# Wide attentions of a four-layer transformer trunk on one core: a batch's output projection a slot later, values made ahead of turning the outputs

## The reference

```python
def _L1_xattn_ref(q, kv, Wq, Wk, Wv, Wo, bo):
    qh = (q @ Wq).reshape(B, N, NUM_HEADS, HEAD_DIM).transpose(0, 2, 1, 3)
    kh = (kv @ Wk).reshape(B, M, NUM_HEADS, HEAD_DIM).transpose(0, 2, 1, 3)
    vh = (kv @ Wv).reshape(B, M, NUM_HEADS, HEAD_DIM).transpose(0, 2, 1, 3)
    attn = jax.nn.softmax(jnp.einsum('bhnd,bhmd->bhnm', qh, kh) * scale, axis=-1)
    out = jnp.einsum('bhnm,bhmd->bhnd', attn, vh)
    return out.transpose(0, 2, 1, 3).reshape(B, N, INNER) @ Wo + bo

def _mha(x, y, ..., causal):                      # layer 2, twice
    xn, yn = _ln(x, lnx_g, lnx_b), _ln(y, lny_g, lny_b)
    a = jax.nn.softmax(jnp.einsum('bhsd,bhtd->bhst', q, k) * D ** (-0.5), axis=-1)
    if causal:
        a = a * (jnp.arange(t)[None, :] > jnp.arange(s)[:, None])
    o = jnp.einsum('bhst,bhtd->bhsd', a, v)
    x_out = x + o.transpose(0, 2, 1, 3).reshape(..., H * D) @ li1_w + li1_b
```

## Time and profile before

| | |
|---|---|
| time, median of 3 runs | 1491.01 us (1490.46 to 1492.49) |
| time of the profiled execution | 1502.04 us |
| its span, first to last instruction | 1500.3 us |
| mean granted clock of TensorE | 0.812 of full speed |
| busy: PE, DVE, ACT, POOL | 1046.5, 916.3, 693.2, 628.5 us |
| L1x, L2a1, L2a2 in the span | about 283 to 496, 602 to 809, 864 to 1037 us |

### The profile page before, as it was taken

One profiled execution on the slowest core, in us unless ns is written; L12 is line 12 of the kernel. 1 busy time (PEld: TensorE's weight loads), 2 busy tenths in 40 slices (PEclk: granted clock), 3 DMA queues, 4 the chain that ended last, 5 costly groups with the idle time before them and its releaser, 6 DMA issues.

```text
span 1500.3 us, 37065 instructions
## 1 busy us (share of the span) xinstructions
PE 1046.5 (70%) x14701; PEld 800.4 (53%) x14748; DVE 916.3 (61%) x2387; ACT 693.2 (46%) x1356; POOL 628.5 (42%) x575
## 2 busy tenths in 40 slices
PE   0477777688888454688885678886827992667674
PEld 0355566456677243366673447674516781445564
DVE  5567554677765694789865566653615456767443
ACT  2546454565553442554433455543514553555321
POOL 3355724164343333355342245442144036655333
PEclk9768588899999675799975868995857995678797
DMA  6533132110010100000000000000022123332122
GB/s 167 140 111 94 59 81 69 38 43 21 23 31 9 33 16 32 19 16 10 3 3 35 2 1 3 3 3 1 1 69 64 52 62 109 106 111 77 48 66 79
DMA packets 68790, 71.54 MB, mean 48 GB/s; under 512 B 11598, under 2 KB 51918, under 8 KB 68430
## 3 DMA queue, kind: packets, MB, share of 16 engines
q1 hardware_dynamic: 64528, 60.77, 14.2%
q0 software_dynamic: 4096, 8.40, 1.9%
HBM read 44.90 MB, written 23.59 MB: 46 GB/s over the span
## 4 chain that ended last, share of the span: by engine, by line
PE 48%; DVE 26%; ACT 9%; issue 7%; POOL 4%; DMA 3%; POOLq 2%; SPq 1%; ACTq 0%; DVEq 0%
PE psum L631 20%; PE psum L1100 6%; PE psum L1118 5%; DVE area L1699 5%; PE psum L750 5%; PE psum L740 4%; ACT area L1189 2%; PE psum L638 2%; POOL sorted_in L2563 2%; ACT xn L1211 2%; DVE area L1805 2%; DVE negm L1798 2%; DVE stats L1680 2%; POOLq L2373 1%; DVE area L1909 1%
## 5 line engine op out<-in xcount | busy, mean ns | idle before, releaser
L1189 ACT ACTIVATE area<-psum 128x512 bf16<-128x512 f32 (+4 forms) x288 | 148.2, 543 | 225.6 <-PE psum L785 103.2
L1699 DVE TENSOR_TENSOR area<-psum,area 128x512 bf16<-128x512 f32 (+3 forms) x280 | 163.2, 622 | 43.8 <-ACT area L1189 43.0
L2434 POOL TENSOR_TENSOR area<-area 77x1024 bf16<-77x1024 f32 x64 | 121.6, 1916 | 98.3 <-ACT area L1322 98.3
L631 PE MATMUL psum<-area 77*128 77x65 bf16 (+4 forms) x3712 | 133.8, 189 | 22.2 <-DVE area L2093 21.6
L1322 ACT ACTIVATE area<-psum 77x1024 f32<-77x1024 f32 (+1 forms) x96 | 97.7, 1021 | 103.0 <-PE psum L750 102.8
L1798 DVE TENSOR_REDUCE negm<-psum 128x4 bf16<-128x308 f32 (+1 forms) x192 | 95.5, 539 | 80.6 <-PE psum L723 80.6
L631 PEld LDWEIGHTS psum<-area 77*128 77x128 bf16 (+2 forms) x3712 | 124.7, 104 | 29.9 <-issue 25.0
L2292 DVE TENSOR_TENSOR area<-area 128x512 bf16<-128x512 f32 x106 | 73.1, 691 | 108.7 <-ACT area L1595 79.7
L1100 PE MATMUL psum<-xT_hi,moe 128*128 128x128 bf16 x848 | 110.3, 228 | 15.7 <-DVE xT_lo L1699 11.6
L638 PE MATMUL psum<-wide,xn 128*128 128x128 f32 x144 | 32.2, 367 | 113.2 <-ACT xn L1211 100.5
L2392 POOL TENSOR_TENSOR moe<-stage,moe 128x512 bf16<-128x512 f32 x47 | 55.5, 1183 | 131.6 <-ACT moe L1184 131.4
(11 more groups left out here) (226 smaller groups left out, 2619.3 us busy)
## 6 DMA issues: line engine op xcount, KB each, us to landing
area<-keys_dram SPq DMA_DIRECT2D x24, 320.0 KB, 5.0
area<-sorted_in SPq DMA_DIRECT2D x22, 256.0 KB, 3.6
sorted_out<-area SPq DMA_DIRECT2D x22, 256.0 KB
keys_dram<-area SPq DMA_DIRECT2D x8, 640.0 KB, 3.0
stage<-in_w_L0m SPq DMA_DIRECT2D x16, 256.0 KB, 2.9
stage<-in_w_L2m SPq DMA_DIRECT2D x16, 256.0 KB, 2.7
stage<-in_w_L3m SPq DMA_DIRECT2D x16, 256.0 KB, 3.0
area<-queries_dram SPq DMA_DIRECT2D x24, 128.0 KB, 2.6
```

The costliest lines, as they stand in the source:

```text
L631: ins = pe.matmul(out, lhsT, rhs, start=i == 0, stop=i == len(terms) - 1)
L1189: ins = act.activation(out, bank, ACT.Copy)
L1699: ins = dve.tensor_tensor(out, bank, high, ALU.subtract)
L2434: pool.tensor_tensor(A.PL[n % 4][0:A.L], A.PF[n % 4][0:A.L, :].rearrange("p (h q) -> p h q", h=8), A.PH[n % 4][0:A.L], ALU.subtract).then_ ...
```

## The change

In the wide attentions the output projection of a batch is issued one slot later, behind the first pair of row maxima, and the last one behind the loop; the values are made (TensorE) and split (ScalarE, VectorE) ahead of the turned outputs. In VectorE's program of L2a1 the values also come ahead of the low half of the first exponentials. GpSimd's and SyncE's programs are as they were.

```diff
@@ tensor_program, attention @@
             if b < B:
                 row_maxima(b, (0, 1))
+            if b >= 5:
+                out_project(b - 5)
             if 0 <= b - 3 < B:
                 outputs(b - 3)
+            if 0 <= b - 1 < B:
+                values(b - 1)
             if b >= 4:
                 turn_outputs(b - 4)
-            if 0 <= b - 1 < B:
-                values(b - 1)
             if b < B:
                 row_maxima(b, (2, 3))
             if ahead < NG and b % GB >= 1:
                 for kind, tile in A.jobs_at(b):
                     project(ahead, kind, tile)
-            if b >= 4:
-                out_project(b - 4)
             if ahead < NG and b % GB == 0:
                 group_turned(ahead)
             if ahead < NG and b % GB == 1:
                 keys_turned(ahead)
+        out_project(B - 1)
         end()
```

## The result

The changed kernel took 1508.36 us (median of 4 runs, 1504.94 to 1511.07) against 1491.75 for the kernel before (1490.46 to 1495.17): a ratio of 1.0107, 95% interval 1.0075 to 1.0138. It is 16.6 us slower, where 6.3 us of gain were forecast. The profiled execution is its fastest, 1504.94 with a span of 1502.9. The order of TensorE, VectorE and ScalarE moved as the diff says; L631, L638, L723, L740 and L785 keep their numbers, the others stand one or two further down: `copy_hi` is L1190, `split_lo` L1700, xn L1212, the maxima L1799, the exponentials' low half L1806, GpSimd's mask L2444.

What follows compares the result with a forecast made beforehand. Bound: TensorE and VectorE handing work to and fro, neither full. -(3.2 + 1.2 + 2.6) - 2.7 + 5.9 - 2.7, given as -6.3, took the median of 1491.0 to 1484.7 us; range 1476 to 1495.

Steps and rivals of the forecast that it cites:

- rival 4: Whole kernel: slower because TensorE's clock falls to 1.2 GHz behind stalls, 2.2 us a drop; chance 0.17.
- six turning slots: Slots b = 4 and 8 of the three wide attentions, each forecast to stall 1.3 to some 2 us.
- The term of 5.9: Slots b = 4 and 8: the projection no longer covers ScalarE's late xn; 5.9 us lost (2.1 + 2.3 + 1.5).
- 2.2 a drop: Price of one clock fall, read from an L2a1 slot at 0.55 that took 11.36 us against 9.17.
- Ordinary slots: b = 12 to 15, without projections: gains of 3.2 us in L2a2, 1.2 in L1x, 2.6 in L2a1.
- M: Second pair of maxima; in L1x forecast still to wait about 0.75 to 0.8 us for the values' second low half.
- the loop through GpSimd: L2a1's ordinary slots: outputs, low halves, exponentials and masks form a binding loop of 8.8 us, down from 9.17.
- T in L1x: Turning of batch b-4's outputs; its first low half, ending 1.97 us after its products begin, was applied to L2a1's values.
- b = 16: Slot without maxima: waits of 1.13 us in L2a2, 0.86 in L1x and 0.7 in L2a1 vanish; sum 2.7.
- The wait for xn: Turning of xn at b = 4 and 8: TensorE waits for ScalarE's normalised xn, 1.3 us (L1x) to some 2.
- Slots with projections: Wide attentions: L1x 0, L2a2 gains 1.4 us, L2a1 1.3 at b = 5 and 9; -2.7 in all.

## Why the prediction was wrong

**The step that failed** is the weighing of rival 4. The prediction had written the mechanism and its outcome with all six turning slots, 1498, and gave it 0.17, because "1.50 in every slot of L2a1 did not bring it in the 106 us ahead of it". That took a wait that VectorE had imposed in ten slots as a proof that TensorE may stand still so long anywhere. So the sum held the clock at nothing. The runs showed otherwise: L2a2's b = 9 took 14.18 behind a wait of 2.14 and 9.32 without it, with the wait for xn gone 29 us come back, and with the wait filled 18. The term of 5.9 for the slots that turn the next group was right for L1x's and L2a2's b = 8, left out what follows them, and was 3.6 too small for L2a1's b = 8 alone (13.79 against 9.66, 0.5 forecast), which had a clock of 0.62.

Rival 4 was nearer, but it too tied the falls to the six waits for xn. The measured 1508.36 is above its 1498, and part of the time at the lower level stands elsewhere: L2a1's b = 3 (0.51) comes ahead of its first such wait, the fall in b = 8 ahead of the second, and b = 14 to 16 (0.83 to 0.86) six slots and more behind the last. With the swap alone the clock fell with no wait for xn at all, and with the projection's move alone the kernel is not slower. A small slip stands beside this: the terms of the sum add up to -6.5, not -6.3.

**Its size** was off too. "2.2 a drop" was read from a slot of L2a1 (11.36 against 9.17) in which TensorE had 1.5 of waiting to give up to the lower clock. L2a2's b = 9 holds projections and had 8.4 of work in 9.74, so half the clock cost 4.4; L1x's b = 9 lost 1.5 (15.05 against 13.53), with a clock of 0.89.

The Trainium skill, TensorE: Matmul & The Clock Gate, section "HAM oscillation", lets the clock fall behind idle gaps; L2a2's b = 9 agrees, though the gap of 2.14 there is shorter than the waits of the section's example (3 to 5 us, for a DMA). L2a1's b = 8, at 0.50 with no wait above 0.91 in the 10 us ahead of it, does not show such a gap.

**Ordinary slots.** L2a2: 6.56 with no wait, forecast 6.6. L1x: 9.44 with 0.85 ahead of M, forecast 9.43 and 0.75 to 0.8. Both right, 4.6 us of gain (4.4 forecast). L2a1: the loop through GpSimd binds and TensorE waits 1.02 inside the outputs, as said, but the loop is 9.16 and not 8.8. The terms of it that were too small: V's low half ends 2.22 behind the start of its products (756.03 to 757.56 + 0.69), where I took 1.97 from T in L1x, since V is three products summed in one bank and ScalarE starts 0.90 behind the first, not 0.72; some 0.1 more lies in two hand-overs between VectorE and GpSimd. Besides, b = 12 took 8.52, not 7.67. So the new order won 0.7 there instead of 2.6 even at full clock, and b = 14 and 15 (10.27 and 10.00) were not at full clock. The second exponentials ended 1.08 behind the mask that they met (753.51 against 752.43), the length taken from the earlier trace rows; by the full block of the Trainium skill's SBUF — State Buffer, "SBUF: two separate sides", it would have been 1.21, and here as there the row is a little shorter.

**b = 16**: 6.19 in L2a2 against 8.15 (the wait of 1.13 gone, most of the rest a stretch at the lower level in the kernel before), 8.03 in L1x against 9.07, a gain of 1.04 where 0.86 was forecast. Near enough there; in L2a1 9.28 against 9.23, with 2.6 us at the lower level, so nothing of the 0.7.

**The wait for xn**: 1.34 in L1x (forecast 1.35), 2.14 in L2a2, 2.08 in L2a1; L1x's and L2a2's slot 8 longer by 1.06 (11.28 against 10.22) and 0.87, forecast 1.05 and 0.95. Right to a tenth in these two.

**Slots with projections** (forecast -2.7): L2a2's b = 6, 7, 10 and 11, at full clock, were shorter by 0.18, 0.46, 0.16 and 0.17, and b = 9, where xn early kept the clock up, by 0.42: 1.4, as forecast. L2a1 won nothing on the whole: b = 3 took 11.53 against 9.88 before, b = 9 with xn early 12.13 against 12.54, b = 10 11.43 against 11.10. That b = 3 is ahead of any turning and is 9.88 again once the exponentials' low half goes first. The swap has a part in it, which I had put at zero: b = 2 took 11.96 in all profiles with the values ahead of the exponentials, 10.85 in most of the others, and b = 3 was at 0.51 behind it. But with the projection's move alone b = 3 was at 0.57 too (11.19), so that the swap is not shown to be the only cause.

**What is shown and what not.** Shown: the wait for xn costs the new order more than the whole loss, and mostly through the clock and not through its length; the wait alone, without the swap, does not make the kernel slower; and the swap costs L2a1 more than it gives (with the projection late in both, L2a1 took 172.6 with the swap and 156.8 without; with xn early its stretch and the projection outside it came to 160.6, against 159.1 before and 154.2 with the low half first). Open: what a wait must be like to bring a fall. Its length does not tell: 1.92 in the old order's L2a2 left the next slot alone and 2.14 in the new one's did not; 1.34 in L1x lowered b = 9 (15.05) and not b = 5 (13.57), which it did lower (14.98) in another run of the same program for L1x. Nor is it shown why the clock fell at the start of L2a1's b = 8, with the filler too and not with xn early, why wait and swap together cost L2a1 so much more than either, or how the 18 and 29 us divide between falls of the clock and its coming back later.

## What to carry to other kernels

When a step is moved away from in front of a wait, price the wait twice: its own length, and the next TensorE-bound slot at half clock (4.4 us here for a wait of 2.1). That second price is a risk and not a certainty: the same wait brought it in some places and not in others. Then look for what is late, and move that too: four activations a group issued earlier turned +1.1% into -0.9%. To tell the clock from the wait, fill the wait with work that computes nothing; if the time comes back while the slot stays as long, it was the clock. And where a change has two parts, measure each alone: here neither half nor the wait told the whole.

## What the hardware showed that was not expected

- One wait of 2.14 us at the end of a slot that was otherwise full was followed by 14.18 us at a granted clock of 0.52, though TensorE was busy 13.93 of them: the lower level did not end as soon as the work was there again.
- Work that computes nothing counts: 14 float32 transposes, 1.75 us, in place of most of that wait (0.76 was left, ahead of them) went with a clock of 1.00 through the next slot, 9.31 in place of 14.18.
- The length of the wait alone does not order the cases: 1.92 and 1.34 (L1x, b = 4) without a fall behind them, 1.34 (L1x, b = 8) and 2.14 with one. And the same order with the same wait of 1.34 (L1x, b = 4) was followed by 13.57 us at 1.00 in one profile and 14.98 at 0.90 in another. Where in time the wait lies may be what matters; that was not tried.
- A fall needs no long wait just ahead of it: L2a1's b = 8 in the changed kernel was at 0.50 from its start, 11 us ahead of its wait for xn, and L2a2's b = 8 with the swap alone was at 0.50 throughout (12.62 us against 8.33).
